# First attention hop of a graph network: rows multiplied out of PSUM, three of seven tiles by ScalarE, thirty index fetches moved behind the last hop

## The reference, cut to what matters

```python
A = (1.0 - ALPHA) * att                      # a weight per edge and head
Z0 = entity_embed[:, None, :]
Z_init = jnp.broadcast_to(Z0, (N_ENTITIES, HEADS, DIM))
def step(Z, _):
    msgs = A[:, :, None] * Z[tail_ids]
    Z_new = jax.ops.segment_sum(msgs, head_ids, num_segments=N_ENTITIES) + ALPHA * Z0
    return (Z_new, None)
Z, _ = jax.lax.scan(step, Z_init, None, length=POW_ITER)
out = Z.reshape(N_ENTITIES, HEADS * DIM) @ W_o
```

## Time and profile before

| what | value |
|---|---|
| median of three runs | 10783.97 us (10775.03 to 10790.59) |
| the profiled execution | 10765.98 us, span 10764.2 us |
| GpSimd busy over the span | 68% |
| VectorE busy over the span | 63% |
| TensorE, ScalarE busy over the span | 53%, 27% |
| first hop: first load issued, closing scatter L1480 | 2158.4, 2571.12 us |
| last hop: last gather, next GpSimd operation | 4772.60, 4817.77 us |

### The profile page before, as it was taken

How to read it: one execution, slowest core, us unless ns; L and a number is a source line. 1 busy time by engine, 2 the same in 40 slices (tenths; PEclk the granted TensorE clock), 3 DMA queues, 4 the chain that set the end, 5 groups by cost and what they waited for, 6 DMA issues and landing times. The chain is left out here.

```text
span 10764.2 us, 113652 instructions
## 1 busy us (share of the span) xinstructions
PE 5684.9 (53%) x26903; PEld 4008.1 (37%) x26903; DVE 6764.3 (63%) x14006; ACT 2874.5 (27%) x5217; POOL 7275.2 (68%) x7087
## 2 busy tenths in 40 slices
PE   3756999300000002877777776766764569622255
PEld 1453323000000001765555564555553447522234
DVE  8954333495878787987676666877775766411127
ACT  0042222001222223443333543222221322100045
POOL 3855777487777777767676765767777767677720
PEclk9978999655555555877777776777665655555578
DMA  0064333153545454437766665654445989511158
GB/s 14 4 235 121 73 71 73 20 196 107 166 145 168 145 165 133 128 118 210 203 211 198 204 204 178 231 165 139 133 132 167 314 219 125 86 46 46 46 197 242
DMA packets 1454719, 1555.31 MB, mean 144 GB/s; under 512 B 1037505, under 2 KB 1158687, under 8 KB 1454490
## 3 DMA queue, kind: packets, MB, share of 16 engines
q1 hardware_dynamic: 1191816, 1284.78, 37.6%
q0 software_dynamic: 252160, 248.38, 12.6%
q10 hardware_dynamic: 10514, 19.71, 0.5%
HBM read 883.57 MB, written 800.52 MB: 156 GB/s over the span
## 5 line engine op out<-in xcount | busy, mean ns | idle before, releaser
L2602 POOL DMA_INDIRECT r_got<-state,comb_src x1176 | 1187.9, 1010 | 431.0 <-issue 344.3
L312 POOL DMA_INDIRECT payload_or_bias_rows<-payload,place x784 | 938.6, 1197 | 484.5 <-issue 254.6
L1797 PE MATMUL hop_ps_into<-hop_out,span_s 128*128 128x256 f32 x8 | 4.9, 714 | 2054.1 <-DVE hop_out L1620 2054.1
L1446 POOL DMA_INDIRECT hop_got<-edges_b,next_col x784 | 829.7, 1058 | 261.4 <-issue 237.6
L1446 POOL DMA_INDIRECT hop_got<-edges_a,next_col x784 | 784.6, 1001 | 259.4 <-issue 238.2
L1797 PEld LDWEIGHTS hop_ps_into<-hop_out,span_s 128*128 128x128 f32 x8 | 2.0, 310 | 2056.4 <-DVE hop_out L1620 2056.4
L1684 ACT COPY hop_got<-hop_zeros 128x1792 f32<-128x1792 f32 x224 | 378.1, 1688 | 1116.0 <-DVE hop_ps_msg L1571 1106.5
L1620 DVE SCALAR_TENSOR_TENSOR hop_out<-hop_out,hop_runs_now,hop_ps_msg 128x256 f32<-128x256 f32 x1176 | 565.6, 481 | 50.9
L2882 PE MATMUL r_ps_v<-dense1g,r_gt 128*128 128x128 f32 x3136 | 588.9, 361 | 0.0
L2882 PEld LDWEIGHTS r_ps_v<-dense1g,r_gt 128*128 128x128 f32 x3136 | 534.8, 264 | 134.2 <-issue 134.2
L2702 DVE SCALAR_TENSOR_TENSOR r_acc<-r_acc,r_runs_now,r_got 128x64 f32<-128x64 f32 x1173 | 334.7, 285 | 278.4 <-DMA r_got<-state,comb_src 235.3
(11 more groups left out here) (816 smaller groups left out, 17759.0 us busy)
## 6 DMA issues: line engine op xcount, KB each, us to landing
edges_a<-hop_out SPq DMA_DIRECT2D x112, 896.0 KB
edges_b<-hop_out SPq DMA_DIRECT2D x112, 896.0 KB, 4.3
r_in<-state SPq DMA_DIRECT2D x168, 448.0 KB, 4.5
hop_side<-x_dst SPq DMA_DIRECT2D x280, 224.0 KB
own<-plain_y SPq DMA_DIRECT2D x56, 952.0 KB
x_and_sums<-c_y SPq DMA_DIRECT2D x56, 896.0 KB, 5.1
bn_in<-x_and_sums SPq DMA_DIRECT2D x56, 896.0 KB
r1a_in<-own SPq DMA_DIRECT2D x84, 448.0 KB, 4.6
```

The source lines that it names most:

```text
L312: nc.gpsimd.indirect_dma_start(out=t.raw[:, n, :], out_offset=None, in_=t.pay[k], in_offset=bass.IndirectOffsetOnAxis(t.place[:, k, n:n + ...
L1446: pool.indirect_dma_start(out=got[:, u, c, :], out_offset=None, in_=table, in_offset=at, bounds_check=EP - 1, oob_is_err=False).then_inc(g ...
L2602: pool.indirect_dma_start(out=got[:, n, c - b * CT, :], out_offset=None, in_=table, in_offset=bass.IndirectOffsetOnAxis(idx[:, at + c:at + ...
```

## The change

Three edits, all in the attention layer.

1. In the first hop ScalarE copies the unit's rows from `hop_side` to PSUM (`hop_ps_side`), and VectorE's multiply reads them from there.
2. VectorE's multiply covers the first four tiles of a unit. The other three (`BY_SCALAR`) are multiplied by ScalarE out of `hop_side`, one activation of 128 x 64 for each tile and head, the weight as a scale per partition. VectorE waits for them in front of its fifth link (`act_part`). `hop_side` is free for the next load when ScalarE is done with it.
3. The first hop issues 212 fetches instead of 242; the other 30 (`AFTER_LAST_HOP`) are issued behind the gathers of the last hop. hop1 to hop3 keep 16 each, with other tile numbers.

```diff
+AFTER_LAST_HOP = 30
+BY_SCALAR = 3
...
+    begins = kind == "heads" and table is None
...
             if table is None:
-                payload_rows(nc, t, 1, range(UNDER_FIELDS + UNDER_WEIGHTS + 6 * UNDER_SCAN, TILES - 3 * AFTER_HOP), t.got_t)
+                payload_rows(nc, t, 1, range(UNDER_FIELDS + UNDER_WEIGHTS + 6 * UNDER_SCAN, TILES - 3 * AFTER_HOP - AFTER_LAST_HOP), t.got_t)
...
+            if after is not None:
+                payload_rows(nc, t, 1, after, t.got_t)
             if rows_too:
                 return
-            if after is not None:
-                payload_rows(nc, t, 1, after, t.got_t)
...
-                            past(sp, side_scaled if banks else msg_ready, i, u, 2)
+                            past(sp, act_part if begins else side_scaled if banks else msg_ready, i, u, 2)
...
-                            m = msg[:, u % 2].rearrange("p c (h d) -> p c h d", h=H)
-                            nc.vector.tensor_tensor(m, four(sides[:, u % 2]), att, ALU.mult).then_inc(msg_ready[u], 1)
+                            here = CT - BY_SCALAR
+                            m = msg[:, u % 2, 0:here].rearrange("p c (h d) -> p c h d", h=H)
+                            copied = ps_side[:, u % 2, 0:here * D].rearrange("p (c d) -> p c d", c=here)
+                            att = t.att_e[:, :, bass.ds(order(i, u) * CT, here)].rearrange("p h c -> p c h").unsqueeze(3)
+                            dve.wait_ge(side_scaled[u], i + 1)
+                            nc.vector.tensor_tensor(m, copied.unsqueeze(2).to_broadcast([P, here, H, D]),
+                                                    att.to_broadcast([P, here, H, D]), ALU.mult).then_inc(msg_ready[u], 1)
...
+                        if begins and c == CT - BY_SCALAR:
+                            dve.wait_ge(act_part[u], i + 1)
...
+                    if begins:
+                        act.wait_ge(side_in[u], (i + 1) * 16)
+                        past(act, msg_ready, i, u, 2)
+                        nc.scalar.copy(ps_side[:, u % 2, 0:CT * D], sides[:, u % 2].rearrange("p c d -> p (c d)")).then_inc(side_scaled[u], 1)
+                        for c in range(CT - BY_SCALAR, CT):
+                            for h in range(H):
+                                ins = nc.scalar.activation(msg[:, u % 2, c, h * D:(h + 1) * D], sides[:, u % 2, c, :], ACT.Copy,
+                                                           scale=t.att_e[:, h, bass.ds(order(i, u) * CT + c, 1)])
+                        ins.then_inc(act_part[u], 1)
...
-        first = TILES - (4 - k) * AFTER_HOP
+        first = TILES - AFTER_LAST_HOP - (4 - k) * AFTER_HOP
...
-    edge_pass(nc, t, "hop4", "heads_out", t.runs_s, t.span_s, t.fix_node_s, table=tables[1], idx=t.next_col, target=t.own1)
+    edge_pass(nc, t, "hop4", "heads_out", t.runs_s, t.span_s, t.fix_node_s, table=tables[1], idx=t.next_col, target=t.own1,
+              after=range(TILES - AFTER_LAST_HOP, TILES))
```

More of the change, by code:

```diff
@@ L1364, in edge_pass @@
         if banks:
-            ps_m, ps_side = psum("ps_msg", [P, 4 * 512]), psum("ps_side", [P, 2, 512])
+            ps_m = psum("ps_msg", [P, 4 * 512])
+        if banks or begins:
+            ps_side = psum("ps_side", [P, 2, 512])
         add = None if rows_too else sb("add", [P, O])
@@ L1394, in edge_pass @@
         linked, blank, added = sem("linked"), sem("blank"), sem("added")
-        runs_ready, side_scaled, zeroed = sems("runs_ready"), sems("side_scaled"), sems("zeroed")
+        runs_ready, side_scaled, zeroed, act_part = sems("runs_ready"), sems("side_scaled"), sems("zeroed"), sems("act_part")
         rt_done, rt_read, gt_done, gt_read, lin_done = sem("rt_done"), sem("rt_read"), sem("gt_done"), sem("gt_read"), sem("lin_done")
@@ L1554, in _ @@
                         dve.wait_ge(gathered[u], (i + 1) * 16 * CT)
-                    if side is not None and not banks:
+                    if side is not None and not banks and not begins:
                         dve.wait_ge(side_in[u], (i + 1) * 16)
```

## The result

| what | before | after |
|---|---|---|
| median, run side by side | 10781.95 us (10775.03 to 10790.59) | 10684.47 us (10679.02 to 10690.15) |
| the profiled execution, its span | 10765.98, 10764.2 us | 10681.55, 10679.8 us |

The ratio is 0.9909, with a 95% interval of 0.9892 to 0.9926, so 80 to 116 us were saved; the medians differ by 97.5. A second set of five rounds gave 10663.05 against 10765.16 us, ratio 0.9912 [0.9898, 0.9925].

A forecast was written before the change was run, and what follows sets the result against it. GpSimd was taken to set the first hop's end, 93 us behind VectorE. 10765.98 less 112.6 saved there, last hop costing 0, gave 10653.4; with 18.0 to the median, 10671 us, range 10645 to 10708.

The forecast's parts named there:

- GpSimd was the bound, and the PSUM read frees it: First hop: GpSimd ends 93 us behind VectorE; reading PSUM, the multiply holds no fetch, so 212 fetches end at 2441.
- the two pairs of the earlier trace: L1571 and L2789, VectorE work reading PSUM and SBUF; fetches beside them took 1.00 and 0.95 us, taken as no hold.
- The rival that GpSimd still sets the end: First hop: links or the PSUM multiply still hold fetches; L1480 at about 2488, 83 us saved, 10701; chance 0.12.
- The multiply, 1.22 us; the activations, 3.07: First hop, per unit: VectorE's multiply shrinks to 1.22 us; ScalarE's twelve activations take 0.256 each, 3.07, in time by 0.2.
- The row of 0.256: Nearest profile row for one ScalarE activation, 0.256 us alone, from which twelve were priced at 3.07 us.
- The load path binds in every second unit: First hop: 5.6 us from a unit's last link to the multiply of the unit after the next; two units take 10.46.
- The last hop costs 0: Last hop: the 30 moved fetches end at 4814, covered by SyncE's last store, issued until 4813.88; cost 0.
- What the sum left out: The sum: L1480 moves from 2571.1 to 2458.5, 112.6 us saved in the first hop, with 0 lost in the last.

The follow-up runs named there:

- the first experiment: Kernel before plus only the copy to PSUM: VectorE multiplies all seven tiles from there, no fetch moved; 10714.98 us, one run, beside 10790.66 before.

## Why the prediction was right, point by point

**GpSimd was the bound, and the PSUM read frees it.** Right, shown by the first experiment and its reverse, the multiply from SBUF. Of the two pairs of the earlier trace rows that stood for it, only the first tells anything: the fetch of 4847.94 ended at 4848.89, and held to 0.82 behind the end of L2789 (4848.05) it would have ended at 4848.87, so held and free look alike there. The fetches take 0.997 us on average; with gaps 1.32 (1.33 forecast), and they ended at 2437.5 (2441). The rival that GpSimd still sets the end falls. The Trainium skill, "SBUF — State Buffer", section "Who interferes with whom", lets the links hold fetches too. The rows agree with a short hold: the fetch of 2402.62 ends at 2403.68, and that of 2406.48 at 2407.55, 0.82 behind the ends of links (2402.86, and 2404.17 plus five links, some 2406.7), as the held ones ended 0.82 behind the multiply. But a link lasts 0.49, so such a hold ends with that link and costs little: 71 of the 134 fetches that start under a link took over 1.0 us, the longest 1.21. That is not the three link steps that the rival supposed.

**The multiply, 1.22 us; the activations, 3.07.** Right: 1.224 and 2.97. The sum was right from a wrong part: 0.333 each, not 0.256, made up by overlap, which is luck. The row of 0.256 squares one tile and has no weight per partition. No link waited for ScalarE.

**The load path binds in every second unit.** Right in mechanism: the experiment with loads early takes it away and lands at 4.87. 34 of the 56 multiplies waited for the copy, somewhat more than every second one. The size was 5.6 us from last link to multiply; in the timeline above it is 2408.57 - 2402.86 = 5.71, of which store to copy 4.78 (4.79 in the forecast: 2404.66 to 2409.45), copy to multiply 0.68 where 0.55 stood for the copy alone, without the handover to VectorE. From the first multiply to the end of the last link it took 295.9 us (2159.8 to 2455.7) for 292.1. The multiply started 1.8 us earlier than forecast and the store landed 0.1 sooner, which leaves the 1.9 by which the scatter was late; that the early start hid half of the miss is luck.

**The last hop costs 0.** Off by 2.0 us. The step named SyncE's last store as cover; the fetches ended under it, at 4704.48, but GpSimd's closing still lies behind them. Its drain there, before the change and after it:

```profile
L1347 POOLq DRAIN  x1: 22284/22284/22284, 4759.7 to 4759.7; - x1
```

```profile
L1350 POOLq DRAIN  x1: 19979/19979/19979, 4688.7 to 4688.7; - x1
```

It ended at 4782.0 before, long ahead of the last store, and at 4708.7 after, behind it. Its end, not that of the last fetch, was to be compared with the store's. In the whole stretch from the second hop's first load to x_fix the 2.0 do not show (2240.0 us before, 2236.9 after; 2236.6 and 2235.4 on the chip of the five rounds).

**What the sum left out.** The handover to the second hop became 6.8 us longer (6.62 to 13.43). No step spoke of it: the forecast took it that what follows the scatter moves with it. At x_fix the two profiles differ by 107.0 us from the span's start, where the forecast had 112.6.

**The rest to 97.5.** The profiled executions differ by 84.4 us, though at the last stage before the second Chebyshev pass they still differed by 111.9. The windows of that pass, from its first scatter (`cheb_rows`) to the next x_fix, in the profile before, then after:

```profile
8754.50:9301.20 546.70, 460.44 (x1906) 394.76 (x1906) 353.00 (x844) 128.31 (x392) 380.58 (x393) 0.51 0.87 121
```

```profile
8642.60:9217.30 574.70, 460.83 (x1906) 395.23 (x1906) 352.21 (x844) 129.24 (x392) 379.17 (x394) 0.51 0.87 115
```

The same work, and 28 us more. On the chip of the five rounds, before and then after:

```profile
8743.40:9301.90 558.50, 460.73 (x1906) 395.22 (x1906) 352.27 (x844) 129.01 (x392) 378.27 (x393) 0.51 0.86 118
```

```profile
8626.60:9185.80 559.20, 463.79 (x1906) 397.78 (x1906) 352.31 (x844) 128.80 (x392) 379.11 (x393) 0.50 0.85 118
```

558.5 and 559.2: there the change leaves the pass alone. Neither value had been expected (565 to 585 or some 547 before, some 575 after). So the 28 us are not the change's, and a difference of two single executions is no measure of it; the stages of the first hop are, since they repeat within 1 us (410.1 and 409.9; 300.6 and 300.3). The length of the pass seems to go with the chip: the four profiles on the chip of the five rounds have 557.3 to 559.2, the six on two other chips 572.4 to 584.9, and the chip of the first two profiles is not on record. The cause was not tried. Stage sums give 104 to 106 us at x_fix (2656.8 - 2551.0; 2653.1 - 2549.1); the medians, 97.5 and 102.1, hold this within their intervals.

## What to carry to other kernels

When two engines share a stretch, the second one's chain must be priced before the first is freed: two edits worth 86 and 41 us alone gave 110 together with a third, since each only helps until the other engine ends last. A new step between a load and its user lengthens the whole path from the release of the buffer, and where that path is longer than the work of the units in between, an earlier load gives it back (23 us here). GpSimd, given work behind its last gathers, was done when its closing drain ended (4708.7), not when the last fetch did (4704.48): cover for such work has to reach that far.

## What the runs showed of the hardware that was not expected

- The drain at the end of GpSimd's block in the first hop lasted 0.30 to 8.88 us, with the number of indirect fetches ahead of it: 0.082 us more for each, and 8.6 us less with 228 than with 220. The other edits did not change it (8.22 in all six profiles with 212, 1.44 in all three with 242). Why is open.
- A fetch held by a VectorE instruction with two inputs from SBUF ended 0.82 us behind that instruction, whether it lasted 2.02 us (fetch 2.67), 1.23 (1.80) or 0.49 (1.06). Not all that start under one are held: in the changed kernel 63 of the 134 that start under a link took 1.0 us or less.
- Activations of 128 x 64 with a scale per partition last 333 ns each in the profile, and twelve in a row 2.97 us; the one without it took 256.
